# A transformer tower on one core: finishing steps moved among the bursts of the first attention, and the last layer's token tiles ordered by batch with the results added among the tiles

## What is computed

```
h = x @ W + positions
h = h + layernorm(attention(layernorm(h)) + layernorm(h))   # 8 heads of 16, whole sequence
h = h + sequence_moe(layernorm(h))    # 8 experts, 2 chosen for a batch by pooled gates
h = h + block_attention(layernorm(h)) # a token attends to those at its place in 32 blocks of 32
h = h + token_moe(layernorm(h))       # 8 experts, 2 chosen for each token
```

## Time and profile before

| | |
|---|---|
| median of 3 runs | 1395.64 us |
| the profiled execution: its own time | 1399.67 us |
| its span, first to last instruction | 1397.9 us |
| mean granted clock of TensorE | 0.916 |
| busy over the span: TensorE, ScalarE, VectorE, GpSimd | 1188.1, 996.6, 934.3, 563.1 us |
| first exponential to last | 49.5 to 618.2 us (512 of them, mean 1034 ns) |
| first row load of the token experts | 1082.29 us |
| last scatter issued, first load of results | 1354.67, 1360.84 us |

### The profile page before, as it was taken

The page is one execution under the profiler, slowest core; times in us unless marked ns, Lnnn a source line. Parts: engine busy times, 40 slices in busy tenths (PEclk is TensorE's granted clock), DMA queues, the critical chain, the costliest instruction groups (busy, mean ns, idle before and its releaser), DMA issues. The chain is left out here.

```text
span 1397.9 us, 26985 instructions
## 1 busy us (share of the span) xinstructions
PE 1188.1 (85%) x9386; PEld 794.3 (57%) x9386; DVE 934.3 (67%) x2612; ACT 996.6 (71%) x1351; POOL 563.1 (40%) x546
## 2 busy tenths in 40 slices
PE   3799999999999998979989997888971999999930
PEld 2344444444444444437768875777861788888830
DVE  4466868686868686748978885777652566666625
ACT  0598888888888888858868986455420899999930
POOL 3423434333333333210201100177776277776760
PEclk9799999999999999979999999889865899999975
DMA  3673737464645455223211300011115667767619
GB/s 86 121 188 91 190 90 180 99 178 101 172 107 159 117 148 127 84 88 111 86 61 61 100 22 8 5 51 47 49 48 171 208 234 238 245 233 256 218 31 355
DMA packets 93164, 180.58 MB, mean 129 GB/s; under 512 B 15597, under 2 KB 64200, under 8 KB 84960
## 3 DMA queue, kind: packets, MB, share of 16 engines
q1 hardware_dynamic: 73664, 129.97, 33.3%
q0 software_dynamic: 17344, 42.68, 9.3%
q10 hardware_dynamic: 2016, 6.16, 1.4%
HBM read 116.96 MB, written 63.12 MB: 129 GB/s over the span
## 5 line engine op out<-in xcount | busy, mean ns | idle before, releaser
L744 ACT ACTIVATE a_probs<-a_psS 128x1024 f32<-128x1024 f32 x512 | 484.3, 1034 | 93.6 <-PE a_psS L829 59.7
L841 PE MATMUL a_psO<-a_probs,a_v 128*32 128x256 f32 x4096 | 282.9, 395 | 16.9 <-DVE a_o_t L1018 16.5
L1257 DVE TENSOR_TENSOR f_g_lo<-f_g,f_g_hi 128x512 fp32r<-128x512 f32 x284 | 195.2, 689 | 117.4 <-ACT f_g L1163 115.8
L2051 POOL DMA_INDIRECT result<-f_out,f_idx x156 | 181.5, 1164 | 93.7 <-issue 58.7
L841 PEld LDWEIGHTS a_psO<-a_probs,a_v 128*32 128x32 f32 x4096 | 108.9, 111 | 154.2 <-issue 89.7
L1639 POOL DMA_INDIRECT queue<-all_row,all_idx x128 | 126.3, 987 | 38.5 <-issue 37.9
L829 PE MATMUL a_psS<-ag_qs,ag_ks 50*128 50x512 f32 x512 | 97.4, 457 | 9.4 <-issue 5.8
L829 PE MATMUL a_psS<-a_qs,a_ks 50*128 50x512 f32 x512 | 97.4, 456 | 7.5 <-issue 3.5
L402 POOL TENSOR_TENSOR ag_rs_f<-ag_veps_f,all_half 128x4 f32<-128x4 f32 x32 | 33.7, 1054 | 125.9 <-DVE ag_veps_f L99 125.9
L1418 POOL TENSOR_TENSOR ah_rs<-ah_veps,all_half 128x4 f32<-128x4 f32 x16 | 18.5, 1155 | 156.1 <-DVE ah_veps L1431 156.0
L829 PEld LDWEIGHTS a_psS<-ag_qs,ag_ks 50*128 50x128 f32 x512 | 39.9, 191 | 57.4 <-ACT a_probs L744 31.3
(11 more groups left out here) (370 smaller groups left out, 2866.2 us busy)
## 6 DMA issues: line engine op xcount, KB each, us to landing
all_w<-experts SPq DMA_DIRECT2D x19, 1026.5 KB, 5.3
experts<-a_split POOLq DMA_DIRECT2D x32, 512.0 KB, 4.9
ag_qs<-experts SPq DMA_DIRECT2D x14, 1026.5 KB, 5.4
ag_ks<-experts SPq DMA_DIRECT2D x14, 1026.5 KB, 5.2
all_rows<-queue SPq DMA_DIRECT2D x39, 260.0 KB, 5.4
f_w<-experts SPq DMA_DIRECT2D x8, 1026.5 KB, 5.3
qparts<-a_parts SPq DMA_DIRECT2D x16, 512.0 KB, 3.6
kparts<-a_parts SPq DMA_DIRECT2D x14, 512.0 KB, 3.2
```

Source lines behind the costliest of these rows:

```text
L744: nc.scalar.activation(probs[u % NPR][:, :], psS[score_buffer(u)][:, :, :].rearrange("p a n -> p (a n)"), ACT.Exp).then_inc(exp_done, 1)
L841: last = nc.tensor.matmul(psO[32 * g:32 * g + 32, a * HALF:(a + 1) * HALF], v[par][:, 2 * hp + p, kt, :], probs[u % NPR][:, cols:cols + HA ...
L1257: nc.vector.tensor_tensor(g_lo[i][:, n, :], g[:, n, :], g_hi[i][:, n, :].bitcast(F32), ALU.subtract).then_inc(lo_done, 1)
L2051: pool.indirect_dma_start(result, bass.IndirectOffsetOnAxis(ap=idx[i][:, j:j + 1], axis=0), out[i][:, j, :], None, bounds_check=2 * B * S ...
```

## The change

Four things.

In the first attention the tables are changed. Splits move from bursts 7, 15, 22 and 27 to 10, 14, 22 and 30 (not in the last batch). Finishing steps move: moments of the first half from burst 2 of the next batch to burst 31 of its own, second from 4 to 2, score from 6 to 4; add_bias of the second half from 10 to 15, normal 12 to 17, moments 18 to 23, second 23 to 25, score 25 to 27. In the last batch the moments of the first half stay where they were, in the next stage. The rescue's branch, on TensorE ahead of the scores of units 53 and 54, now stands between them; its rare path uses one bank in place of two.

The plan orders the tiles by the batch in which each first gets a row. TensorE sums the counts of each batch up to it and before it (16 products with a new small input, `since`), VectorE works on 8 partitions, one for each batch, and one more product adds them. After min(4(b+1)+7, 39) tiles all rows of batches 0 to b are done (FULL).

The results are added during the token experts, seven tiles behind (LAG): at tile FULL[b]+7, that is 18, 22, 26, 30, 34, 38 for batches 0 to 5, SyncE stores batch b-1 and loads batch b in two DMAs, behind that tile's weights; VectorE adds at the same tile, one choice at n=0 and one at n=2. Batches 6 and 7 come behind the last tile, batch 7 in halves on two queues. The buffers are ones that stand free. The block of its own and GpSimd's last waits go.

```diff
-    SPLIT = [{7: 0, 15: 1, 22: 2, 27: 3}] * (B - 1) + [{5: 0, 12: 1, 16: 2, 21: 3}]
+    SPLIT = [{10: 0, 14: 1, 22: 2, 30: 3}] * (B - 1) + [{5: 0, 12: 1, 16: 2, 21: 3}]
...
-    FREE = (score_buffer(2 * RESCUE), score_buffer(2 * RESCUE + 1))
-    UPPER = {2: ("moments", 0), 4: ("second", 0), 6: ("score", 0), 10: ("add_bias", 1), 12: ("normal", 1), 18: ("moments", 1), 23: ("second", 1),
-             25: ("score", 1)}
-    LOWER = {26: ("add_bias", 0), 28: ("normal", 0)}
+    FREE = score_buffer(2 * RESCUE + 4)
+    UPPER = {2: ("second", 0), 4: ("score", 0), 15: ("add_bias", 1), 17: ("normal", 1), 23: ("moments", 1), 25: ("second", 1), 27: ("score", 1)}
+    LOWER = {26: ("add_bias", 0), 28: ("normal", 0), 31: ("moments", 0)}
+    KEEP = (26, 28)
...
-                    if m in LOWER:
+                    if m in LOWER and (more or m in KEEP):
...
-                    if more and m == RESCUE:
-                        rescue(b + 1, 1 - par, uses.next())
-                        uses.count -= 1
                     for u in (2 * m + 3, 2 * m + 4):
                         if u < UNITS or more:
                             scores(b, par, u)
+                        if more and u == 2 * RESCUE + 3:
+                            rescue(b + 1, 1 - par, uses.next())
+                            uses.count -= 1
...
             nc.tensor.matmul(psS[:, 0:E], all_ones[:, :], counts[:, :], start=True, stop=True).then_inc(n_ps, 1)
+            for i in range(2):
+                for n in range(B):
+                    last = nc.tensor.matmul(psX[0][0:B, i * E:(i + 1) * E], since[:, i, n, :], newc[:, n, :], start=(n == 0), stop=(n == B - 1))
+            last.then_inc(n_ps, 1)
+            pe.wait_ge(sums_done, 1)
+            nc.tensor.matmul(psX[1][0:1, 0:2 * N], all_ones[0:B, 0:1], both_f[:, :, :].rearrange("b i m -> b (i m)"), start=True, stop=True).then_inc(tile_ps, 1)
...
+class Adds:
...
+        self.FULL = [min(self.K * S // CH * (b + 1) + N - self.K * B * S // CH, N) for b in range(B)]
+        self.LAG = 7
+
+    def load(self, eng, b, parts=(0, 1)):
+        rows = self.result[b * self.K * self.S:(b + 1) * self.K * self.S, :].rearrange("(p k t) d -> p k t d", p=P, k=self.K)
+        for i in range(2):
+            eng.wait_ge(self.sent[i], (self.FULL[b] + 1 - i) // 2 * 16 * TPC)
+        if b >= 2:
+            eng.wait_ge(self.summed, b - 1)
+        for k in parts:
+            eng.dma_start(self.y[b % 2][k][:, :, :], rows[:, k, :, :]).then_inc(self.y_in[b % 2], 16)
...
+    def sync(self, sp, m):
+        for b in range(self.B - 2):
+            if m == self.FULL[b] + self.LAG:
+                if b:
+                    self.store(sp, b - 1)
+                self.load(sp, b)
+
+    def sync_end(self, sp):
+        B = self.B
+        self.load(sp, B - 2)
+        self.store(sp, B - 3)
+        self.store(sp, B - 2)
+        self.load(sp, B - 1, (0,))
+        self.store_half(sp, B - 1, 0)
+        sp.wait_ge(self.stored, (B + 1) * 16)
+
+    def act_end(self, act):
+        self.load(act, self.B - 1, (1,))
+        self.store_half(act, self.B - 1, 1)
...
+    def dve(self, dve, m, n):
+        for b in range(self.B - 2):
+            if m == self.FULL[b] + self.LAG:
+                if n == 0:
+                    self.add(dve, b, 0)
+                elif n == 2:
+                    self.add(dve, b, 1).then_inc(self.summed, 1)
...
             for m in range(2, N):
                 load_rows(m)
                 load_parts(m)
+                adds.sync(sp, m)
+            adds.sync_end(sp)
...
-            for i in range(2):
-                pool.wait_ge(sent[i], len(range(i, N, 2)) * 16 * TPC)
...
-        add_results(nc, H, result, out, B, S, D)
+        token_experts(nc, H, queue, result, out, (shared.n0, ahead.f), rows, rows_in, tile_e, tile_row, experts[1], w1, w1_in, B, S, D)
```

More of the change, by code:

```diff
@@ L1285, in _ @@
         back(N - 1)
+        if aside is not None:
+            aside.close(dve)
 class Rest:
@@ L1962, in plan @@
                 dve.drain()
-                nc.vector.tensor_tensor(over[:, :, :], ends[:, :, :].broadcast_to([1, N, E]), number[:, :].unsqueeze(2).broadcast_to([1, N, E]), ALU.is_le)
+                nc.vector.tensor_scalar(ends[:, 0, :], ends[:, 0, :], open_[:, :], None, ALU.add)
                 dve.drain()
-                nc.vector.tensor_reduce(e_f[:, :], over[:, :, :], AX, ALU.add)
-                nc.vector.tensor_tensor(part[:, :, :], over[:, :, :], tiles[:, :, :].broadcast_to([1, N, E]), ALU.mult)
+                nc.vector.tensor_tensor(begin[:, :, :], ends[:, :, :], fresh[:, :, :], ALU.subtract)
@@ L1974, in plan @@
-                nc.vector.tensor_scalar(done_f[:, :], e_f[:, :], float(STRIDE), None, ALU.mult)
+                nc.vector.tensor_tensor(off[:, :, :], off[:, :, :], base[0:B, :, :], ALU.add)
+                count = number[:, :].unsqueeze(2).broadcast_to([B, N, E])
+                nc.vector.tensor_tensor(over[:, :, :], ends[:, :, :].broadcast_to([B, N, E]), count, ALU.is_gt)
+                nc.vector.tensor_tensor(part[:, :, :], begin[:, :, :].broadcast_to([B, N, E]), count, ALU.is_gt)
                 dve.drain()
-                nc.vector.tensor_tensor(row_f[:, :], row_f[:, :], done_f[:, :], ALU.add)
+                nc.vector.tensor_tensor(over[:, :, :], over[:, :, :], part[:, :, :], ALU.subtract)
@@ L1977, in plan @@
                 dve.drain()
-                nc.vector.tensor_scalar(row_f[:, :], row_f[:, :], float(E * STRIDE), None, ALU.min)
-                nc.vector.tensor_scalar(e_f[:, :], e_f[:, :], float(E - 1), None, ALU.min)
+                nc.vector.tensor_reduce(hits[:, :], over[:, :, :], AX, ALU.add)
+                nc.vector.tensor_tensor(part[:, :, :], over[:, :, :], off[:, :, :].broadcast_to([B, N, E]), ALU.mult)
                 dve.drain()
-                nc.vector.tensor_copy(tile_row[:, :], row_f[:, :])
@@ L1982, in plan @@
-                nc.vector.tensor_copy(tile_e[:, :], e_f[:, :])
+                nc.vector.tensor_reduce(both_f[:, 0, :], part[:, :, :], AX, ALU.add)
+                nc.vector.tensor_tensor(hits[:, :], hits[:, :], number[:, :], ALU.mult)
+                dve.drain()
+                nc.vector.tensor_tensor(part[:, :, :], over[:, :, :], number[:, 0:E].unsqueeze(1).broadcast_to([B, N, E]), ALU.mult)
+                nc.vector.tensor_scalar(hits[:, :], hits[:, :], float(CH), None, ALU.mult)
+                dve.drain()
@@ L2011, in token_experts @@
+def token_experts(nc, H, queue, result, out_rows, y, rows, rows_in, tile_e, tile_row, ident, parts, w, w_in, B, S, D):
     E, _, WIDE = parts.shape
@@ L2162, in tower @@
             block_attention(nc, H, queue, counts, row, idx, sent, rows, rows_in, tile_e, tile_row, experts[1], w1, w1_in, ident, half, ahead, ins, B, S, D)
-        token_experts(nc, queue, result, rows, rows_in, tile_e, tile_row, ident, experts[1], w1, w1_in, B, S, D)
-        add_results(nc, H, result, out, B, S, D)
+        token_experts(nc, H, queue, result, out, (shared.n0, ahead.f), rows, rows_in, tile_e, tile_row, ident, experts[1], w1, w1_in, B, S, D)
 def host(inputs):
@@ L2202, in host @@
     a["place_of"] = (np.arange(128)[:, None, None] * K * t + np.arange(K)[:, None] * t + np.arange(tiles) // t * K * S + np.arange(tiles) % t).astype(np.int32)
-    a["upto"] = np.tril(np.ones((8, 8), np.float32))[None]
-    a["steps"] = (np.arange(M) * CH).astype(np.float32)[None, None]
-    a["number"] = np.arange(N).astype(np.float32)[None]
+    a["upto"] = np.tile(np.tril(np.ones((8, 8), np.float32)), (b, 1, 1))
+    a["steps"] = np.tile((np.arange(M) * CH).astype(np.float32), (b, 1, 1))
+    a["number"] = np.tile(np.arange(N).astype(np.float32), (b, 1))
+    first, then = np.meshgrid(np.arange(b), np.arange(b), indexing="ij")
+    a["since"] = np.tile(np.stack([first <= then, first < then]).astype(np.float32), (128, 1, 1, 1))
     a["pad_place"] = np.tile((K * b * S + np.arange(128)).astype(np.int32)[:, None, None], (1, 4, 1))
```

141 lines of the change are left out of this document (84 added, 57 removed).

## The result

The changed kernel takes 1379.08 us in the median (1376.45 to 1380.20, 4 runs) against 1396.22 for the kernel before in the same session: a ratio of 0.987, 95% interval 0.985 to 0.990. It is faster by 17 us, where 39 were forecast, and lies above the range. Its profiled execution took 1379.24 us, with a span of 1377.3 (before 1397.9), so 20.6 us of span are to be explained.

A forecast was written before the change was run, and what follows sets the result against it. Bounds: uncovered end (42.2 us), late transposes at the first attention's pair changes, TensorE in the token experts. Attention 15, plan 0, tiles -3, end 27 make 39: 1399.67 to 1360.7, less 4.0 for the median, 1356.6 us; range 1343 to 1374.

The forecast's parts named there:

- Pair changes: First attention, behind bursts 7 and 15: steps moved off VectorE's late transposes end stalls and clock falls; 22.5 us gained.
- the 4 us named: Sign in the profile after: waits of a_psO for VectorE's transpose at pair changes come under 4 us.
- the floor of 0.29: ScalarE's idle time at a pair change where VectorE is punctual; both late changes were to fall to 0.29 us.
- The rescue test: First attention, burst 25: with the branch between the two scores, one exponential can run under it; 2.5 us gained, bounds 0 and 7.
- What is late next: First attention, burst 21: TensorE waits for GpSimd's k square behind the stream, six batches; 10 us lost, bounds 0 and 15.
- The rival of exchanged waits: First attention: moved steps make squares, divides and later steps as late as pair changes were; gain 0, 1371.6 us, chance 0.2.
- Results among the tiles: Token experts: results' transfers in SyncE's queue delay the next rows up to 4.6 us; 3 us lost, bounds 0 and 26.
- The head-of-line rival: Token experts: rows have no room, TensorE pays for every transfer of results; 26 us lost instead of 3, 1379.6 us, chance 0.12.
- The plan: Behind the last route: the longer plan is covered by the last scatters into the queue; cost 0.
- The end: Behind the last scatter: only the last batch remains to load, add and store; 27 us gained, bounds 22 and 32.

The follow-up runs named there:

- experiment 5: Experiment 1 with the rescue test put back ahead of both scores of burst 25: 1366.14 us, ratio 0.979.
- experiment 7: Experiment 1 with ScalarE instead of SyncE issuing the results' loads and stores among the tiles: four executions, 1364.88 to 1376.14 us.
- experiment 8: Experiment 1 without the five stores among the tiles, so batches 0 to 4 are not written; its time is not in the text.
- experiment 1: The changed kernel with GpSimd's square of the second k chunk ahead of the stream of the second half: 1363.79 us, ratio 0.975.
- experiment 11: Experiment 1 with a third buffer for rows, so each tile's rows are loaded a tile earlier: 1354.88 us, ratio 0.972.
- experiment 9: The kernel before with only the new tables of the first attention and the later rescue test: 1396.39 us, ratio 1.001.

## Why the prediction was wrong

*Pair changes: the mechanism right, the size by luck.* 22.5 us were forecast; the trace has 22.4 at the two changes in batches 1 to 6, and the wait for the transpose fell under the 4 us named (0.6). But the 22.5 were nine tenths of 20.1 for waits and of 5 for the clock, so 18.1 and 4.5, and the parts came out otherwise. The clock's five falls were there, and cost more: in the trace of before the change that a fall follows costs 1.6 us more than the same change without one in batches 2 and 3, and 2.0 more in batches 4 to 6, 9.3 in all. The waits gave the other 13.1, near the 13.4 by which ScalarE's wait for the second products fell (31.7 to 18.3): it stands at 0.40 each in 46 places now, and not at the floor of 0.29. Two errors of some 5 us cancel.

One reason why the old stretches were late was read as a price and is an encounter. Add_bias took 1.58 us and the subtraction L945 1.78 in the earlier trace rows because of where they stood: in the trace of before six of sixteen add_bias take 1.58, each beside a square on GpSimd, and six of sixteen subtractions 1.41 to 1.79, each beside the stream; all the others take 0.69. After the change none does:

```profile
366.50 0.69 DVE L945 TENSOR_TENSOR a_nT_lo<-a_nT,a_nT_hi 128x512 fp32r<-128x512 f32 x1
369.38 0.69 DVE L435 TENSOR_TENSOR ag_res<-ag_res,ag_brow 128x512 f32<-128x512 f32 x1
```

So beside being moved, VectorE's work shrank by 0.9 and 1.1 us a batch, which no term of the prediction had.

*The rescue test: mis-sized, and its part not shown.* 2.5 us were put on one exponential running under the branch. The place gave 6.9, and with the test put back the attention is no longer (551.5 us against 551.8); whether the stall that now stands one burst ahead hides the test's cost stays open (experiment 5).

*"What is late next": the step that failed.* The place was named, burst 21 and k's square behind the stream, in six batches. The size was not: minus 10, with 15 as its bound, and it is minus 28.6. Counted from the end of the q product (373.48 in batch 4): the normalising ends at 4.4 and not 3.7, because reading and splitting q took 2.4 us and not 2.1 and the normalising 1.87; GpSimd then idles 0.65 us between the first two operations of the stream and takes 4.9 us for it, not 4.0 (its operations were added up without what lies between them, and the second takes 1.54 and not 1.3); the square ends at 10.3 and not 8.9. So the wait is 2.75 us, twice the 1.4 forecast: 16.5 instead of 8.4. And the clock: I took two falls of 1 us. There were five in six batches, and each cost more. Batch 4, the one without a fall, loses 2.9 us at bursts 23 to 25, batches 5 and 6, with a fall of 3.3 us, 4.3 each, and batches 1 to 3, with one of 6.7 us, 5.7: so 1.3 us for the short fall and 2.8 for the long one, 11 of the 28.6 us, where 2 were put. The Trainium skill's rule that VectorE and GpSimd exclude each other (SBUF — State Buffer, "SBUF: two separate sides") would have made it 15 and not 10. The trace agrees with the rule where VectorE's operation starts second: its subtraction beside the stream took 1.78 us before, 0.69 without the stream. At the place priced here VectorE's split of k started first, and took its 0.69; the stream's second operation took 1.54 us where 1.28 is usual. So the rule was worth some 0.3 us a batch here, 1.6 in six, and not 5.

The error is one of bounds too. The bound of 15 had room neither for a wait twice as long nor for the clock's answer to it: ScalarE was idle for 2.85 us here against 1.65 and 2.14 at the pair changes of before, and even behind the second of these the clock fell. The rival of exchanged waits (0.2, 1371.6) was the right one for the attention: it gained 1 us in the trace, and the tables alone measured 1.001.

*Results among the tiles: mis-sized, 9.6 instead of 3.* The rows were to come up to 4.6 us late, and came 5.0 late; but half of this is not the bytes. They are issued 2.53 us later than otherwise, since SyncE is issuing the three transfers, and take 7.88 us from issue to reading instead of 5.4. The room before VectorE waits is 1.75 us, as the earlier trace rows showed (1.7), and VectorE waits 3.25. Behind that two rooms were counted, 0.87 of idle time and 1.2 "since it works a step ahead", 2.07 in all; the trace has about 1.5. At the load alone VectorE waits 1.38 us and no tile is late; at the next three transfers it waits 3.25, 3.81 and 3.41, and the tiles are late by 1.73, 2.34 and 1.90, each some 1.5 less (the f_x_lo that TensorE's next transposes wait for stands close behind the late copy). So the room is 3.25 and not 3.8, and the rows come 5.0 to 5.6 us late and not 4.6: about 2.0 us a point and not 0.8. The fourth point has 3.67, and 1.6 of it, by the starts of TensorE's transposes from tile to tile, is a fall of the granted clock behind its stop of 1.91 us, which stood in no sum. And five points were counted where four can make a tile late: behind the transfers at tile 38 no rows follow.

The head-of-line rival (26 us) overshot for the reason given against it: there is room, 3.25 us. It had the mechanism; that its 1379.6 lies beside the 1379.08 measured is luck, as it was reckoned with 15 us from the attention, which gave 1. On the rule that a DMA engine works through one queue in ring order and takes turns between queues (the Trainium skill, DMA: Bandwidth & Descriptors, "Queues, rings and completion order"), from which the prediction took that another queue would cost less: on ScalarE's queue the waits for rows fell from 15.5 to 8.6 us, so the trace agrees in direction. The same page's "Issuing engines are not separate DMA queues" says that to issue from another engine only saves the sequencer's time, usually small. Here that time was the 2.5 us by which the rows went out late; on ScalarE it stopped GELU instead, and the kernel was not faster for it, with the reservations of experiment 7.

*The plan: right* (0). *The end: right*, 30.5 for 27, inside 22 to 32.

Together: 39 = 22.5 + 2.5 - 10 - 3 + 27 was forecast. Measured are 22.4 + 6.9 - 28.6 - 1.1 + 1.5 (batches 0 and 7) - 9.6 + 30.5 = 22, of which 20.6 are seen in the span and 17 between the medians. Against 39 the attention lacks 14 and the tiles 7, and the end gave 3.5 more. With the square moved and a third buffer the kernel comes out at 1354.88, where 1356.6 had been forecast for the change as it is.

## What to carry to other kernels

When steps are moved away from one deadline, walk every queue that they now stand in (here GpSimd's, where a stream of 4.9 us came to stand ahead of a square of 1.04 that TensorE waits for), with the idle time between dependent operations and not the operations alone, and count a full stop of TensorE at more than its length.

For a load that is issued as late as its buffers allow, the room is landing to reading and the little that the reader can be late (here 1.75 and 1.5 us); whatever is put in that queue ahead of it, its time of issue included, comes off that. Here one more buffer did more than any rearrangement of the traffic.

And when two errors of a sum could cancel, check its terms one by one in the trace after, and not the sum.

## What the runs showed of the hardware

The time to issue the same transfer varies. A store of 512 KB in runs of 512 bytes took 0.39 to 0.72 us on SyncE; the two loads of results took 0.83 to 0.85 us at five places of experiment 8, and 1.25 to 2.1 us behind a store, but also 1.5 to 1.7 us at tile 18 with no store ahead (kernel after, experiments 1, 8 and 11). What makes the difference stays open.

The clock's answer to the same wait differs. With ScalarE idle for 2.8 to 3.7 us behind this wait in batches 1 to 6, the granted clock went to 0.50 behind five of them (for some 3.3 us in batches 5 and 6, for 6.7 us in batches 1 to 3) and stayed at 1.00 behind one, that of batch 4; in experiment 9 it stayed there in batch 3 alone. In the kernel after, against batch 4, the short fall cost 1.3 us more and the long one 2.8, where the wait itself is 2.75.

VectorE and GpSimd can hold each other up on 128x512 float32 in SBUF: beside one of GpSimd's operations of 1.0 to 1.3 us VectorE's operation with two inputs took 1.58 or 1.78 us where it takes 0.69 alone; where VectorE's started first, it took 0.69 and GpSimd's 1.54 instead of 1.28.
